# Two-layer conditioned FFN on one core: first stage rearranged between ScalarE, GpSimd and VectorE, last weights quantised earlier

## The chip, the cores and the metric

The kernel runs on one core of a Trainium2 chip. The metric is the device time in microseconds of one execution. Each time of a kernel is a median of several executions. A profiled execution is shown with its own time beside it: the span of the trace is a little shorter than the time.

The engines are called TensorE (PE in rows), VectorE (DVE), ScalarE (ACT), GpSimd (POOL) and SyncE (SP, which issues most transfers here). Each has its own instruction queue, executes it in order, and waits on semaphores for the others.

## The reference

x is 128 x 32 x 128 (tokens b, steps t, features c). Four parts follow each other:

1. **Conditioned linear layer**: `out = x W_base^T + b_base`, plus eight low-rank terms (rank 16) weighted by `cond_8` and scaled by 2.
2. **Layer norm, quantised activation and ternary weights**: `xn = (x - mean) * rsqrt(var + 1e-5) * gamma + beta`. The quantisation takes the maximum of |xn| over **all** tokens, divided by 127: nothing behind it can start before all of xn is there. The weights are replaced by `alpha * sign(w)` where |w| is over 0.7 of its mean.
3. **Mixture of experts**: softmax over `cond_8`, the best two of eight experts per token b, each a gated MLP (128 to 512 to 128, gelu), plus one shared MLP for all tokens.
4. **Quantised gated FFN** (128 to 384 to 128): weights in blocks of 32 rounded to 4 bits with their own scale, activations rounded to 16 bits with a scale from the maximum over all values, several times over.

x is added back after part 2 and after part 4. The result is float32.

## The kernel before, in words

The work is written out by hand for each engine (`@block.tensor`, `.vector`, `.scalar`, `.gpsimd`, `.sync`), and the order on each engine is the order of the code. There is no planner. `w.wait_ge(semaphore, count)` is the only link between engines. Even on one engine an operation that reads a predecessor's result waits on its semaphore (`step` counts such results in `d_rt`, `after` waits for them).

**Split values.** Products of float32 are made from `fp32r` halves: `hi` is a rounding copy of the value, `lo = value - hi`, and a product is `hi*hi + hi*lo + lo*hi`. Each weight of the experts (16 pieces of 128 x 512, two per expert) and of the shared MLP (three pieces) is loaded into one of eight staging slots `stg`, split once (`SPLITS`, L250, gives the number of pieces per round), and the 16 expert pieces are stored to a scratch in DRAM (`wscr`, L1745) from a ring of five buffers `wst`. Before, ScalarE made each `hi` (L1372, semaphore `a_whi`) and GpSimd each `lo` (L1601, `k_wlo`). SP waits for each `k_wlo` to store the piece and to reload its slot (L1742 to L1755). The eight down matrices arrive in `wdr`; ScalarE copies them to `WD` (`down_high`, L1331, rounds given by `WDS`), GpSimd makes their low halves (`down_low`, L1605).

**First stage (rounds n = 0 to 11).** Eight blocks of four steps t (128 x 512 values) go through a pipeline with one round per block. In round n TensorE transposes block n, makes the product `z` of block n-2, the low-rank product of block n-1 (`hidden`), the variance of block n-2 and the broadcast of the reciprocal deviation of block n-3. VectorE makes the low half of x (`narrow`), the weighted low-rank values (`hidden`), the maximum of block n-4, the variance plus epsilon (`ST`) and the product of block n-3. ScalarE squares, scales and shifts. GpSimd raises ST to the power -0.5 (L1587), and then makes its halves. Between these, VectorE computes the routing: from two counting products in `bank[6]` it derives the slots of all tokens (`KS`, `RT`, `Pm`, `tmpP`), the list of tiles (`etA` to `etI`) and the thresholds of the ternary weights (`tpos`, `tneg`). Before, most of the routing stands in rounds 2 to 4.

**Barrier.** The maximum of all blocks is reduced on VectorE, turned on TensorE (`turn_max`), reduced again (`top`) and spread (`spread_max`). `busy(k, ...)` are products whose result nobody reads. After that ScalarE rounds xn block by block (`round_xn`, which waits for `d_sc`), and a second pipeline (steps j = 0 to 11) makes the ternary product, adds x, transposes and starts the shared MLP for the first eight of its 32 units. Three products of 128 x 480 give the position table and the slot weights (`p_tab`, L527 to L530), which VectorE copies to `colI` and `Wt` in step 2 (L1048 to L1052). The buffers of the shared MLP (`Gb`, `HbS`) lie over `wst`; those of the transposed x (`XT`) over `stg`.

**Expert tiles and the rest of the shared MLP.** Twenty tiles of 12 or 16 token slots follow (two halves each): GpSimd gathers columns of x (`fetch`, L1622), TensorE makes gate and up products (`unit`) and down products. Then the other 24 shared units (n = 8 to 33). In these, VectorE and GpSimd quantised the last weights `WQ` (VectorE: scale, n = 10 to 12; GpSimd: L1653 to L1661), before TensorE turns them in `WTURN`. `LARGEST` gives the unit in which the maximum of each block is taken.

**Last stage.** The quantised FFN with its maxima over all values (`turn_max` 1 to 5).

## Time and profile before

| | |
|---|---|
| median of 3 runs | 398.12 us (396.21 to 399.63) |
| profiled execution | 397.88 us, span 396.2 us, mean granted clock 0.948 |
| TensorE matmuls, weight loads | 347.5 us (88%), 286.0 us (72%) |
| VectorE | 330.3 us (83%) |
| ScalarE | 262.1 us (66%) |
| GpSimd | 238.9 us (60%) |
| DMA | 47.77 MB, mean 121 GB/s |

Busy shares are averages over stages with different limits. The matmul and the weight load of TensorE overlap. A group of rows names the line of the instruction; L767, L1318 and L1557 are helpers that issue most operations of their engine, so the tiles (out <- in) say what an operation is. "Granted clock" is TensorE's, as a share of 2.4 GHz: 0.5 is 1.2 GHz. In brackets stands how long the engine stood idle before an instruction, and what ended that.

### The profile page before, as it was taken

Reading aid. Unit: us, or ns where it says so; the run is one execution under the profiler, and the core shown is the slowest. Engines: PE = TensorE matmul, PEld = TensorE weight load, DVE = VectorE, ACT = ScalarE, POOL = GpSimd, SP = SyncE. Lnnn points to the kernel's source line nnn. Section 1 sums busy time; section 2 is a strip of 40 time slices with the busy share of each in tenths; the row PEclk is TensorE's granted clock in tenths of the full one; section 3 lists DMA queues with packets and bytes.
Section 4 is the critical chain, followed back from the end, with each engine's and each line's share of the span. In section 5 each row is a group of like instructions: output and inputs, shape, how many; then the busy total and the mean of one; then the engine's idle time right before and its main releaser. Section 6 shows DMA issues by size and latency. Waiting matters only on the chain.

```text
span 396.2 us, 6229 instructions
## 1 busy us (share of the span) xinstructions
PE 347.5 (88%) x1759; PEld 286.0 (72%) x1759; DVE 330.3 (83%) x695; ACT 262.1 (66%) x344; POOL 238.9 (60%) x404
## 2 busy tenths in 40 slices
PE   7988977999999999999999999899999992035997
PEld 6765754768998998989898887688677661022797
DVE  4498667984899999989999989866669699989894
ACT  3656678966656566565756655455556899999760
POOL 2546795897557383756566115832179499994552
PEclk9898999999999999999999999999999996556999
DMA  5997994965244353433532003200000000000022
GB/s 152 346 409 269 331 336 135 296 187 213 106 151 170 112 209 107 174 146 117 201 110 106 2 2 113 100 2 0 1 2 0 1 1 0 0 2 0 1 108 106
DMA packets 19850, 47.77 MB, mean 121 GB/s; under 512 B 2787, under 2 KB 8934, under 8 KB 17254
## 3 DMA queue, kind: packets, MB, share of 16 engines
q1 hardware_dynamic: 18342, 47.16, 34.1%
q10 hardware_dynamic: 1472, 0.20, 0.3%
q8 instruction: 14, 0.23, 0.2%
q14 instruction: 22, 0.18, 0.1%
HBM read 33.10 MB, written 12.58 MB: 115 GB/s over the span
## 4 chain that ended last, share of the span: by engine, by line
PE 56%; POOL 15%; DVE 11%; issue 6%; DMA 5%; ACT 3%; SPq 1%; POOLq 1%; ACTq 0%; DVEq 0%
PE ps L396 55%; POOL G L1698 2%; POOL G L1554 2%; POOL WD L1557 2%; POOL XCh L1554 2%; POOL t L1554 2%; DMA wscr<-wst 2%; DVE O_i L773 2%; DVE unread L1275 2%; DMA wdr<-n_L_cond_skill_down_dram 2%; DMA bsr<-in_L_cond_Bs_dram 1%; PE ps L393 1%; DVE Hl L767 1%; POOL Hl L1557 1%; SPq L1728 1%
## 5 line engine op out<-in xcount | busy, mean ns | idle before, releaser
L1638 POOL CAST xg<-XT 128x64 fp32r x264 | 81.5, 358 | 52.5 <-DVE Hl L767 25.4
L396 PE MATMUL ps<-xg,Wr 128*128 128x384 f32 (+1 forms) x480 | 98.5, 353 | 1.3 <-POOL xg L1638 0.8
L396 PEld LDWEIGHTS ps<-xg,Wr 128*128 128x128 f32 x480 | 85.7, 188 | 8.4 <-POOL xg L1638 1.1
L1318 ACT ACTIVATE Hh<-HbS 128x512 fp32r<-128x512 f32 (+2 forms) x72 | 56.5, 785 | 47.6 <-DVE HbS L767 47.4
L767 DVE TENSOR_TENSOR HbS<-Gb,ps 128x512 f32<-128x512 f32 (+2 forms) x72 | 63.2, 878 | 21.8 <-PE ps L396 18.7
L1318 ACT ACTIVATE Gb<-ps 128x512 f32<-128x512 f32 (+2 forms) x72 | 54.1, 751 | 30.7 <-PE ps L396 28.9
L767 DVE TENSOR_TENSOR Hl<-HbS,Hh 128x768 fp32r<-128x768 f32 (+2 forms) x57 | 59.2, 1038 | 3.5 <-ACT Hh L1318 3.0
L773 DVE SCALAR_TENSOR_TENSOR C<-ps,Wt,C 128x32 f32 x264 | 52.4, 279 | 2.9 <-PE ps L396 2.6
L396 PE MATMUL ps<-XT,SHh 128*128 128x512 f32 x128 | 45.7, 399 | 0.8 <-DVE XT L767 0.4
L1557 POOL TENSOR_TENSOR Hl<-HbS,Hh 128x512 fp32r<-128x512 f32 x15 | 19.5, 1298 | 38.5 <-ACT Hh L1318 38.3
L396 PE MATMUL ps<-Hh,WT 128*128 128x384 f32 (+1 forms) x160 | 37.3, 355 | 0.0
L1318 ACT ACTIVATE ps<-G,S 128x1024 int32<-128x1024 f32 (+3 forms) x35 | 33.3, 987 | 5.4 <-DVE O_i L773 4.2
L396 PEld LDWEIGHTS ps<-Hh,WT 128*128 128x128 f32 x160 | 29.0, 188 | 2.1
L396 PE MATMUL ps<-WFh 128*128 128x512 f32 x30 | 11.4, 516 | 21.1 <-DVE S L776 11.8
L396 PEld LDWEIGHTS ps<-XT,SHh 128*128 128x128 f32 x128 | 24.0, 188 | 6.0 <-issue 0.7
L776 DVE TENSOR_REDUCE S<-G 128x1 f32<-128x1024 f32 (+2 forms) x25 | 28.1, 1166 | 0.3
L1557 POOL TENSOR_TENSOR wst<-stg,wst 128x512 fp32r<-128x512 f32 x16 | 20.6, 1306 | 7.7 <-ACT wst L1318 7.7
L396 PE MATMUL ps<-XT,SHl 128*128 128x512 f32 x64 | 25.0, 391 | 0.0
L396 PEld LDWEIGHTS ps<-WFh 128*128 128x128 f32 x30 | 6.2, 234 | 24.8 <-DVE S L1275 12.1
L396 PE MATMUL ps<-Hl,WT 128*128 128x384 f32 (+1 forms) x80 | 23.1, 370 | 0.2 <-DVE Hl L767 0.2
L396 PEld LDWEIGHTS ps<-WFd,G 128*128 128x128 f32 x192 | 21.7, 192 | 0.9 <-issue 0.9
L396 PE MATMUL ps<-WFd,G 128*128 128x128 f32 x192 | 22.0, 276 | 0.4 <-POOL G L1554 0.3
(223 smaller groups left out, 705.8 us busy)
## 6 DMA issues: line engine op xcount, KB each, us to landing
Wr<-wscr SPq DMA_DIRECT2D x20, 1024.0 KB, 4.9
wscr<-wst SPq DMA_DIRECT2D x16, 512.0 KB, 5.4
stg<-n_L_cond_skill_gate_dram SPq DMA_DIRECT2D x8, 256.0 KB, 6.2
stg<-in_L_cond_skill_up_dram SPq DMA_DIRECT2D x8, 256.0 KB, 6.6
wdr<-n_L_cond_skill_down_dram SPq DMA_DIRECT2D x8, 256.0 KB, 6.1
xscr<-X SPq DMA_DIRECT2D x8, 256.0 KB, 6.1
X<-xscr SPq DMA_DIRECT2D x8, 256.0 KB, 4.4
out_dram<-X SPq DMA_DIRECT2D x7, 256.0 KB, 2.0
```

The lines of the kernel that those rows point to most:

```text
L393: return e.transpose(o_, i_, identF[:, :])
L396: return e.matmul(o_, l, r, start=start, stop=stop, skip_group_check=True)
L767: return e.tensor_tensor(o_, a, b, op)
L773: return e.scalar_tensor_tensor(out=o_, in0=a, scalar=s, in1=b, op0=op0, op1=op1)
L776: return e.tensor_reduce(o_, i_, X, op, apply_absolute_value=absv)
L1275: return e.tensor_tensor_reduce(out=unread[:, p % 2, HALF[h]], in0=sloti(p % 3)[:, HALF[h]], in1=UA[:, p, HALF[h]], scale=1.0, scalar=0.0, ...
L1318: return e.activation(o_, i_, func, **kw)
L1554: return e.tensor_scalar(o_, a, s1, s2, op0, op1)
L1557: return e.tensor_tensor(o_, a, hi.bitcast(F32), SUB)
L1638: last = e.tensor_copy(xg[:, i % XR, :, T * s:T * s + T].rearrange("p a t -> p a t"), XT[:, :, :, bass.ds(regs[s - a_], 1)].rearrange("p a ...
L1698: e.tensor_tensor(Gi[:, pc(p)], Gi[:, pc(p)], t32[:, pooled_nth(f"t{p}") % 2, :], MUL).then_inc(k_y, 1)
L1728: e.dma_start(stg[:, n % 8, :], (sg, su)[n % 2][n // 2]).then_inc(s_stg[n % 8], 16)
```

## The change

- **Splits**: in rounds 1 to 8 twelve pieces (2, 2, 1, 2, 1, 2, 1, 1), both halves on GpSimd, with its own new semaphore `k_whi`. The last seven pieces are split in rounds 9, 10 and 11 (2, 3, 2), high half on ScalarE as before.
- **Down matrices**: their high halves move from rounds 8, 10, 11 and the steps i = 3 to 5 to the steps i = 0 to 5 after the barrier. The transfers have semaphores of their own (`s_wd`).
- **Routing**: the same operations, spread over rounds 3 to 10, ahead of `hidden` of their round. Two table operations with 480 columns (`tmpP`, `iof`) move from GpSimd to VectorE; tmpQ moves to round 10.
- **Table products** stand ahead of the barrier's products, and four instead of eight unread products follow. `colI` is copied between the two reduces of the barrier, `Wt` in step 0.
- **Waits**: rounding waits for the reciprocal alone (`d_inv`). The transposed x waits for single splits instead of all of them on VectorE, not at all on ScalarE.
- **Last weights**: VectorE makes all of their quantisation but one product ahead of the first expert tile, and that product in unit 16.
- **Elsewhere**: the low half of unit 30 is made after the hidden values of unit 31, the maximum of block 6 a unit later, and five unread products ahead of the fourth maximum are gone.

The diff, cut to its core (the routing operations that move are the same text at another place; their new place is given by the round):

```diff
-        SPLITS = (0, 2, 2, 2, 2, 2, 2, 2, 2, 3, 0, 0)
-        LARGEST = {10: 0, 12: 1, 14: 2, 18: 3, 22: 4, 26: 5, 31: 6, 33: 7}
-        WDS = {8: (0,), 10: (1, 2), 11: (3, 4)}
+        SPLITS = (0, 2, 2, 1, 2, 1, 2, 1, 1, 2, 3, 2)
+        NP = sum(SPLITS[:9])
+        LARGEST = {10: 0, 12: 1, 14: 2, 18: 3, 22: 4, 26: 5, 32: 6, 33: 7}
+        WDS = {0: (0,), 1: (1, 2), 2: (3,), 3: (4, 5), 4: (6,), 5: (7,)}
 ... TensorE
-                if n == 6:
+                if n == 8:
                     w.wait_ge(d_place, 2)
                     mm(bank[6][0:1, 0:NSLOT], bcF[:, :], Pm[:, :]).then_inc(p_route, 1)
-                if n == 8:
+                if n == 10:
                     w.wait_ge(d_parts, 2)
                     w.wait_ge(d_ord, 1)
 ...
+            w.wait_ge(d_tab, 1)
+            w.wait_ge(d_var, 8)
+            mm(bank[4][0:1, 0:NSLOT], ones[:, 0:1], tmpQ[:, :]).then_inc(p_tab, 1)
             w.wait_ge(a_zg, 8)
-            busy(8, bank[2], WbTh[:, :], xTh[:, 0, :])
+            w.wait_ge(d_sel, 2)
+            mm(bank[3][:, 0:NSLOT], ones[:, :], tmpP[:, :], True, False)
+            mm(bank[3][:, 0:NSLOT], ones[:, :], iof[:, :], False, True).then_inc(p_tab, 1)
+            busy(4, bank[2], WbTh[:, :], xTh[:, 0, :])
             turn_max(0, bank[6], S[:, 180:181])
             busy(1, bank[2], WbTh[:, :], xTh[:, 0, :])
             spread_max(0, bank[6])
-            (the three table products)
 ... shared_up, shared_down
-                w.wait_ge(k_wlo, NR)
+                w.wait_ge(k_wlo, NR - 1)
 ...
+                w.wait_ge(k_wlo, NR)
 ...
-            w.wait_ge(d_my, 10)
-            busy(5, bank[7], WFh[:, 0, :], WFh[:, 0:4, :].rearrange("p k c -> p (k c)"))
             turn_max(4, bank[7], col(MX2))
 ... VectorE, rounds: routing per round, ahead of hidden(n - 1)
+            3: n_, n_b, n_a (KS)         4: three sums of KS, RT 0 to 2
+            5: RT 3, 4, 6, 5, 4, 5       6: RT 5, 5, 7, S 48, S 56, sum S 42
+            7: bcF, tmpP, Pm             8: tsc, sum, tmpP (d_sel)
+            9: iof (d_sel), ordI        10: tmpQ (d_tab)
+            behind the product of their round: etC 4; tpos, tneg 5; etA, etC, etF 6;
+            tsc, tpos, sum 7; etA, etF, etI 8; tern, alpha 10
 ... VectorE, barrier
             top(0, bank[6])
-            w.wait_ge(k_tab, 1)
-            stt(tmpQ[:, :], vneg[:, :], bcF[:, :], Pm[:, :], ADD, MUL).then_inc(d_tab, 1)
+            w.wait_ge(p_tab, 1)
+            tt(colI[:, :], bank[4][0:1, 0:NSLOT], vneg[0:1, :], SUB).then_inc(d_tab, 1)
 ...
-            step(e.reciprocal(S[:, 183:184], S[:, 182:183]))
+            e.reciprocal(S[:, 183:184], S[:, 182:183]).then_inc(d_inv, 1)
 ...
                     w.wait_ge(a_xt, i + 1)
+                    if i >= 2:
+                        w.wait_ge(k_wlo, min(NG - 1 + i, NR))
                     low(x_half(1, i), bank[5 + i % 3], x_half(0, i)).then_inc(d_xt, 1)
-                if j == 2:
+                if j == 0:
                     w.wait_ge(p_tab, 2)
                     cp(Wt[:, :], bank[3][:, 0:NSLOT]).then_inc(d_tab, 1)
 ... VectorE, ahead of the expert tiles
+            w.wait_ge(s_wq, 48)
+            e.tensor_reduce(Sb, w9, X, ALU.max, apply_absolute_value=True).then_inc(d_bits, 1)
+            ts(Sb, Sb, 1.0 / 7.0, 1e-12, MUL, ALU.max); e.reciprocal(S[:, 104:140], Sb)
+            tt(w9, w9, wide(S[:, 104:140]), MUL); ts(WQ[:, :, :], WQ[:, :, :], RM, RM, ADD, SUB)
 ... VectorE, shared units
-                if n == 31:
-                    shared_low(30)
-                (scale of WQ at n = 10, 11, 12)
+                if n == 16:
+                    w.wait_ge(d_bits, 5)
+                    tt(w9, w9, wide(Sb), MUL).then_inc(d_bits, 1)
 ... ScalarE
-            split = 0
+            split = NP
-                for _ in range(SPLITS[n]):
+                for _ in range(SPLITS[n] if n >= 9 else 0):
 ...
-                w.wait_ge(d_sc, QSC)
+                w.wait_ge(d_inv, 1)
                 do(xnT[:, cols(j)], xnT[:, cols(j)], ACT.Identity, scale=S[:, 183:184], bias=RMC).then_inc(a_q, 1)
 ...
-                    w.wait_ge(k_wlo, NR)
                     do(x_half(0, i), bank[5 + i % 3]).then_inc(a_xt, 1)
-                    if 3 <= i < 6:
-                        down_high(2 + i)
+                    for k in WDS.get(i, ()):
+                        down_high(k)
 ... GpSimd
-                    w.wait_ge(a_whi, split + 1)
+                    if split < NP:
+                        w.wait_ge(s_stg[split % 8], 16 * (split // 8 + 1))
+                        if split >= WRING:
+                            w.wait_ge(s_wst[split % WRING], 16 * (split // WRING))
+                        e.tensor_copy(hi, stg[:, split % 8, :]).then_inc(k_whi, 1)
+                        w.wait_ge(k_whi, split + 1)
+                    else:
+                        w.wait_ge(a_whi, split + 1 - NP)
                     low(lo, stg[:, split % 8, :], hi).then_inc(k_wlo, 1)
 ...
+            w.wait_ge(k_wlo, NR)
             w.wait_ge(d_tab, 3)
             w.wait_ge(p_tab, 2)
             e.memset(C[:, 0:8 * DW], 0.0).then_inc(k_zero, 1)
 ... GpSimd, shared units
-                (the two products and the rounding of WQ at m = 12, 14, 16)
```

## Rows read from the trace of the kernel before

**Rows 1.** Windows: busy us (instructions) per engine, granted clock, DMA share, GB/s.

```profile
26.00:33.40 7.40, 4.80 (x31) 3.70 (x29) 7.33 (x36) 3.87 (x7) 3.89 (x3) 0.99 0.76 298
33.40:40.50 7.10, 7.10 (x32) 4.37 (x31) 6.00 (x14) 3.65 (x6) 3.51 (x3) 0.77 0.95 317
40.50:44.90 4.40, 4.31 (x28) 3.23 (x26) 3.13 (x6) 3.60 (x6) 3.94 (x4) 1.00 0.97 326
```

**Rows 2.** TensorE's timeline: start, busy us, work, [idle before <- releaser].

```profile
31.09 1.05 PE L396 MATMUL ps<-KC,sq 128*128 128x1 f32 x8 [2.60 <-ACT sq L1318]
```

**Rows 3.** ScalarE's timeline, first stage, round 5.

```profile
29.74 0.72 ACT L1318 ACTIVATE xnT<-xnT,S 128x512 f32<-128x512 f32 x1 [2.87 <-DVE xnT L767]
```

**Rows 4.** GpSimd's timeline, first stage: round 2, last power.

```profile
17.79 2.51 POOL L1557 TENSOR_TENSOR wst<-stg,wst 128x512 fp32r<-128x512 f32 x2
...
53.18 1.01 POOL L1587 TENSOR_TENSOR ST<-ST,KC 128x4 f32<-128x4 f32 x1 [0.57 <-DVE ST L770]
```

**Rows 5.** Groups by form, GpSimd, whole span: busy us, mean ns.

```profile
L1638 POOL CAST xg<-XT 128x64 fp32r x264 | 81.5, 358 | 52.5 <-DVE Hl L767 25.4 <-PE ps L396 19.8 <-issue 7.0
L1557 POOL TENSOR_TENSOR wst<-stg,wst 128x512 fp32r<-128x512 f32 x16 | 20.6, 1306 | 7.7 <-ACT wst L1318 7.7
...
L1554 POOL TENSOR_SCALAR XCh<-C,S 128x512 fp32r<-128x512 f32 x8 | 8.2, 1032 | 9.2 <-DVE S L770 9.2
L1587 POOL TENSOR_TENSOR ST<-ST,KC 128x4 f32<-128x4 f32 x8 | 8.1, 1014 | 14.3 <-DVE ST L770 14.3
...
L1554 POOL TENSOR_SCALAR tmpP<-iof,S 128x480 f32<-128x480 f32 x1 | 2.0, 1982 | 0.0
...
L1554 POOL TENSOR_SCALAR vneg<-vint 128x480 f32<-128x480 int32 x1 | 0.6, 594 | 0.0
```

**Rows 6.** VectorE's timeline, first stage, routing.

```profile
18.21 0.88 DVE L767 TENSOR_TENSOR KS<-S 128x8 f32<-128x8 f32 x1
```

**Rows 7.** ScalarE's timeline around the barrier.

```profile
55.29 1.14 ACT L1318 ACTIVATE WD<-wdr 128x512 fp32r<-128x512 f32 x2
...
59.58 0.63 ACT L1318 ACTIVATE WD<-wdr 128x512 fp32r<-128x512 f32 x1 [1.52 <-DMA wdr<-n_L_cond_skill_down_dram]
60.23 1.28 ACT L1318 ACT_TABLE_LOAD   x1
...
61.63 2.91 ACT L1318 ACTIVATE xnT<-xnT,S,S 128x512 f32<-128x512 f32 x4
```

**Rows 8.** TensorE's timeline around the barrier.

```profile
55.15 2.07 PE L396 MATMUL ps<-xTh,WbTh 128*128 128x512 f32 x8
58.09 0.27 PE L393 MATMUL ps<-identF,S 128*1 128x128 f32 x1 [0.86 <-DVE S L776]
...
61.16 0.97 PE L396 MATMUL ps<-iof,ones 128*128 128x480 f32 x2
```

**Rows 9.** VectorE's timeline behind the barrier: position tables.

```profile
66.39 0.63 DVE L767 TENSOR_TENSOR colI<-ps,vneg 1x480 int32<-1x480 f32 x1
66.96 0.64 DVE L764 COPY Wt<-ps 128x480 f32<-128x480 f32 x1
```

**Rows 10.** VectorE's timeline, first expert tile and shared phase.

```profile
86.71 1.47 DVE L767 TENSOR_TENSOR Hl<-HbS,Hh 128x512 fp32r<-128x512 f32 x2
91.94 0.96 DVE L767 TENSOR_TENSOR HbS<-Gb,ps 128x768 f32<-128x768 f32 x1 [3.76 <-PE ps L396]
...
238.53 1.35 DVE L1162 TENSOR_REDUCE S<-WQ 128x36 f32<-128x1152 f32 x1
...
249.66 3.14 DVE L767 TENSOR_TENSOR Hl<-HbS,Hh 128x512 fp32r<-128x512 f32 x1
```

**Rows 11.** TensorE's timeline, shared phase and its end.

```profile
252.86 0.50 PE L396 MATMUL ps<-Hl,SD 128*128 128x512 f32 x1 [1.35 <-DVE Hl L767]
...
284.88 0.73 PE L396 MATMUL ps<-Hh,SD 128*128 128x512 f32 x2 [0.75 <-ACT Hh L1318]
```

**Rows 12.** SP's queue: the last scratch store.

```profile
52.64 0.83 SPq L1745 DMA_DIRECT2D wscr<-wst  x1
```

More of the change, by code:

```diff
@@ L192, in program @@
         s_wst = [sem(f"s_wst{i}") for i in range(WRING)]
+        s_wd = [sem(f"s_wd{i}") for i in range(E)]
         s_wr = [sem(f"s_wr{i}") for i in range(3)]
@@ new lines, in _ @@
+                if n == 4:
+                    n_cum = n_a
+                    for k in range(3):
+                        after(n_cum)
+                        n_cum = step(tt(KS[:, k + 1, :, 4:12], KS[:, k, :, 4:12], KS[:, k, :, 4 - 2 ** k:12 - 2 ** k], ADD))
+                    after(n_cum, n_a)
+                    n_1 = step(stt(RT[:, 0, :], KS[:, 0, 0, 4:12], -16.0, S[:, 72:80], MUL, ADD))
+                    n_2 = step(tt(RT[:, 1, :], KA, KS[:, 0, 0, 4:12], SUB))
+                    n_3 = step(tt(RT[:, 2, :], KB, KS[:, 0, 1, 4:12], SUB))
@@ new lines, in _ @@
+                if n == 5:
+                    after(n_1, n_2, n_3)
+                    n_1 = step(ts(RT[:, 3, :], RT[:, 0, :], 12.0, -28.0, ALU.is_ge, MUL))
+                    n_2 = step(ts(RT[:, 4, :], RT[:, 0, :], 24.0, -28.0, ALU.is_ge, MUL))
+                    n_3 = step(tt(RT[:, 5, :], KA, RT[:, 2, :], ADD))
+                    n_8 = step(stt(RT[:, 6, :], RT[:, 1, :], 16.0, S[:, 72:80], MUL, ADD))
+                    after(n_1, n_2)
+                    n_2 = step(tt(RT[:, 4, :], RT[:, 3, :], RT[:, 4, :], ADD))
+                    after(n_3)
+                    n_3 = step(ts(RT[:, 5, :], RT[:, 5, :], -16.0, 16.0 * (NT - 1), MUL, ADD))
@@ new lines, in _ @@
+                if n == 6:
+                    after(n_2, n_3)
+                    n_3 = step(tt(RT[:, 5, :], RT[:, 5, :], RT[:, 4, :], ADD))
+                    after(n_3)
+                    n_3 = step(stt(RT[:, 5, :], RT[:, 0, :], 0.0, RT[:, 5, :], ALU.is_ge, MUL))
+                    after(n_3, n_8)
+                    n_3 = step(tt(RT[:, 7, :], RT[:, 5, :], RT[:, 6, :], ADD))
+                    after(n_3)
+                    step(tt(S[:, 48:56], S[:, 48:56], RT[:, 7, :], MUL))
+                    n_off = step(tt(S[:, 56:64], S[:, 56:64], RT[:, 7, :], MUL))
+                    after(n_off)
+                    n_tmp = step(red(S[:, 42:44].rearrange("p (k a) -> p k a", a=1),
+                                     S[:, 48:64].rearrange("p (k e) -> p k e", k=2), ADD))
@@ new lines, in _ @@
+                if n == 7:
+                    w.wait_ge(k_const, PART)
+                    cp(bcF[:, :], bcI[:, :]).then_inc(d_place, 1)
+                    after(n_tmp)
+                    n_tmp = step(ts(tmpP[:, :], iof[:, :], S[:, 42:43], None, ALU.is_equal))
+                    after(n_tmp)
+                    stt(Pm[:, :], iof[:, :], S[:, 43:44], tmpP[:, :], ALU.is_equal, ADD).then_inc(d_place, 1)
+                if n == 8:
+                    w.wait_ge(d_parts, 1)
+                    n_ = step(tt(tsc[:, :], tpos[:, :], fwr[:, :], MUL))
+                    w.wait_ge(d_rt, n_)
+                    red(S[:, 47:48], tsc[:, :], ADD).then_inc(d_parts, 1)
+                    w.wait_ge(d_place, 2)
+                    ts(tmpP[:, :], iof[:, :], S[:, 42:43], S[:, 38:39], ALU.is_equal, MUL).then_inc(d_sel, 1)
@@ L857, in _ @@
+                if 2 <= n and n - 1 < 8:
+                    hidden(n - 1)
                 if n == 2:
-                    hidden(1)
                     w.wait_ge(a_rows, 2)
@@ L995, in _ @@
                     ts(ST[:, i % 2, 0:4], AV[:, 0:4], 1.0, 1e-5, MUL, ADD).then_inc(d_var, 1)
[L996 to L1004 removed]
+                scaled(n - 3)
@@ new lines, in _ @@
+                if n == 7:
+                    after(n_)
+                    n_ = step(tt(tsc[:, :], tpos[:, :], tneg[:, :], ADD))
+                    step(tt(tpos[:, :], tpos[:, :], tneg[:, :], SUB))
+                    after(n_)
+                    red(S[:, 46:47], tsc[:, :], ADD).then_inc(d_parts, 1)
+                if n == 8:
+                    after(n_5, n_7)
+                    n_5 = step(tt(etA[:, WIDE:16], etA[:, WIDE:16], etF[:, WIDE:16], SUB))
+                    after(n_5)
+                    n_5 = step(tt(etA[:, WIDE:16], etA[:, WIDE:16], etB[:, WIDE:16], MUL))
+                    step(cp(etF[:, 0:WIDE], etA[:, 0:WIDE]))
+                    after(n_5)
+                    n_et = step(tt(etF[:, WIDE:16], etF[:, WIDE:16], etA[:, WIDE:16], ADD))
@@ L1007, in _ @@
                     ts(etI[:, 1, 0:NT], etF[:, 0:NT], 128.0, None, MUL).then_inc(d_et, 1)
+                if n == 10:
+                    w.wait_ge(p_route, 4)
+                    n_ = step(ts(S[:, 140:141], bank[6][:, 18:19], 1.0, None, ALU.max))
+                    cp(tern[:, :], bank[6][:, 384:512]).then_inc(d_tern, 1)
+                    after(n_)
+                    n_ = step(e.reciprocal(S[:, 141:142], S[:, 140:141]))
+                    after(n_)
+                    n_alpha = step(tt(S[:, 142:143], S[:, 141:142], bank[6][:, 19:20], MUL))
             w.wait_ge(d_mx1, 9)
@@ L1373, in _ @@
                     split += 1
-                for k in WDS.get(n, ()):
-                    down_high(k)
             do(S[:, 11:12], S[:, 13:14], ACT.Gelu_apprx_tanh)
```

218 lines of the change are left out of this document (66 added, 152 removed).

## The prediction

> **What bounds the kernel now.** I read the page's slices first (TensorE is busy almost throughout, except near 30 us and after 285 us), then the windows of the first stage, then each engine's timeline there, and last the waits at the places that the diff touches.
>
> The first stage sends eight blocks of x through rounds 0 to 11 and ends in a maximum over all tokens. The windows [rows 1] show one undisturbed round, 40.50 to 44.90: 4.40 us, TensorE busy 4.31 of it, VectorE 3.13. Four transposes more make it about 4.8 in the rounds that still load a block. The two rounds ahead of it last 7.40 and 7.10 us. In the first of them VectorE is busy 7.33 us: the routing of that round is one burst of small operations. In the second TensorE's granted clock is 0.77, a mixture of 2.4 and 1.2 GHz, just after TensorE has stood idle for 2.60 us [rows 2]. The chain of that idle time is visible: ScalarE waited 2.87 us for VectorE's product [rows 3], and TensorE for ScalarE's square. So some 14.5 - 2 x 4.8 = 4.9 us of the first stage are the price of the burst.
>
> From 94 us to 220 us TensorE is the bound and the change touches nothing.
>
> **Part by part.** *GpSimd takes both halves of 12 splits.* GpSimd starts its round-2 splits at 17.79 and the last power of the rounds at 53.18, done at 54.19 [rows 4]. Between them, in the new schedule, lie 10 split pairs (2,1,2,1,2,1,1 over rounds 2 to 8) and seven powers. A low half is 1.31 us, a power 1.01 [rows 5]. The trace has no plain 128x512 copy to fp32r on GpSimd. From below: a 480-element scalar operation with one input, 0.59. From above: the 480-element one with comparison, 1.98; the strided gather copies, 0.36 for 64 elements, point as high. Nearest, same width and fp32r output: XCh, 1.03 [rows 5]. I take 1.03, plus 0.15 for the wait on its own result. A pair is 2.5, so 10 x 2.5 + 7 x 1.01 = 32.1, and the last power is done at 17.79 + 32.1 = 49.9 instead of 54.2. GpSimd would allow 4.3 us of gain; at 0.59 it would allow all 4.9, at 1.98 it makes the rounds 5.2 us longer.
>
> The GPSIMD Engine Reference of the Trainium skill (section 4.1, Engine selection) advises against such elementwise work on GpSimd for two inputs and calls one input roughly line-rate; its section 3.1 measured 769 ns for 512 elements. By that price, an estimate from the page, the pairs would be 0.26 shorter and GpSimd would not bind at all. No row here shows that operation.
>
> *Routing spread, VectorE beside a fuller GpSimd.* VectorE's own routing work stays, some 13.3 - 2 x 2.5 = 8 us in the two long rounds, now spread over rounds 3 to 10, where about 2 us are free in each. What the spread gives up is GpSimd's silence: the burst ran while GpSimd was waiting. An operation of VectorE with two SBUF inputs that meets a GpSimd instruction ends only when that one ends: the 128x8 minimum at 18.21 took 0.88, until GpSimd's first low half of 17.79 was over [rows 4, 6]. With GpSimd nearly always busy, one such operation passes per GpSimd piece of about 1.2. Round 5 has six and follows a round of two splits: its block is about 2.4 us late, 1.8 of it beyond the slack of 0.6 that the undisturbed round shows between these steps and TensorE. Rounds 3 and 7 (three and two ahead of the block's product) cost 0.2 and 0.9. The rounds that follow one split cost nothing, as GpSimd is through before VectorE needs the port. Sum 2.9. Bounds: none, if they fit in the gaps that GpSimd's own waits leave; all 4.9, if each is held. The rounds give **-4.9 + 2.9 = -2.0 us** (-4.9 to +0).
>
> The same rule has a statement in the GPSIMD Engine Reference (section 1, Specifications): GpSimd's SBUF interfaces are shared with VectorE, with contention for instructions with two SBUF inputs or in a 2-port mode. The trace agrees (0.88 us for eight elements).
>
> *Table products ahead of the barrier.* TensorE is done with the rounds at 55.15 and now has three products of 0.9 (last row 0.97 [rows 8]) and four warm-up products (half of 2.07) before the turn: 55.15 + 2.75 + 1.03 = 58.9, where the turn stood at 58.09. ScalarE's third split of round 10 delays the last shift by 0.5 (two pieces were 1.14 [rows 7]), which lies beside this. Cost 0.8.
>
> *WD halves behind the barrier.* The first rounding waited until 61.63, since ScalarE stood 1.52 us for a wdr transfer, copied it at 59.58 and loaded its table for 1.28 after that [rows 7]. Now two splits (1.1) follow the last shift at 57.8, the table is loaded by 60.3, and the reciprocal is ready at 60.3 too. First rounding at 60.4: **-1.2 us**, the 0.8 included (-0.4 to -1.8).
>
> *colI and Wt.* They sat in VectorE's third step, 0.63 and 0.64 [rows 9]. colI goes into the wait for the maximum, Wt behind the first qT, where about half of it lies in a wait for ScalarE: **-0.7** (-0.3 to -1.2).
>
> *Eight WD copies on ScalarE instead of three, and the quantiser.* Steps 2 and 4 of the pipeline after the barrier get two copies; ScalarE had no slack in step 4, so its high halves, GpSimd's low halves and the first gather come about 0.7 late. Beside this VectorE does the whole quantiser where it had 3.76 us idle ahead of the first expert product at 91.94 (its last low half ends at 88.18 [rows 10]). The reduce is 1.35 [rows 10]; two products and a rounding over as many elements some 0.7 to 1.3 each, small ones 0.3, gaps 0.4, holds 0.5: about 4.9, until 93.1. Both delays overlap: **+1.2** (0 to +2.5), since TensorE has no idle time after it.
>
> *Shared phase.* GpSimd's quantiser goes. It had held VectorE's low half at 249.66 for 3.14 us instead of about 0.7, and TensorE stood 1.35 for it [rows 10, 11]; two smaller holds of the kind cost some 0.4. The one product left for VectorE is covered by its idle time there. **-1.7** (-1.2 to -2.1).
>
> *Its end.* The last product no longer queues behind a low half, so ScalarE's last high half is earlier; TensorE had waited 0.75 for it [rows 11]: **-0.8** (-0.3 to -1.2). The reduce of block 6 moves behind the last low half, still ahead of the last sum. The five warm-up products removed before the fourth maximum ran beside VectorE's reduces: 0. SP's queue keeps its order, later by GpSimd's lag; d_inv and the scalar multiply: 0.
>
> Sum: -2.0 - 1.2 - 0.7 + 1.2 - 1.7 - 0.8 = -5.2. The profiled execution took 397.88, the median is 398.12, 0.24 above. 397.9 - 5.2 = 392.7, as a median 392.9.
>
> **Rivals.** (1) *GpSimd's copy is slow*, near 1.98 [rows 5], decisive from about 1.46, where GpSimd's chain ends at 54.2 as before. Then the rounds cost +5.2 instead of -2.0, and holds by pieces of 2 us add 1 to 3 more: 392.9 + 7.2 + 2 = 402.1, slower. For it: the gather copies' price per element. Against it: XCh. Chance 0.08.
> (2) *The port eats the gain of the rounds*: every two-input operation held, rounds 0, first expert tile +2.0: 392.9 + 2.0 + 0.8 = 395.7. For it: 0.88 for a tiny operation; GpSimd's load rises by 12 copies. Against it: a late VectorE leaves GpSimd idle, which frees the port. Chance 0.24.
> (3) *The last scratch store lands late.* Gb and HbS lie over wst, and the store of split 15 is issued about 4 us later (it was at 52.64 [rows 12]) behind a fuller queue. A landing after 64 would hold the first gelu by up to 3: 394.5 to 396. Chance 0.08.
>
> **How the numbers follow.** The forecast has the remaining 0.60. The sum of all good ends is -11, which needs a copy of 0.6 us and no hold; I set the low end at 388.5. The high end, 399, covers rivals 2 and 3 with their bad ends and half of rival 1. The forecast's own range is 388.5 to 395.5. About 1% (4.0 us) is what a measurement of this kernel tells from no change: faster below 394.1. Forecast mostly there (0.54), a little of rivals 2 and 3 (0.07): faster 0.61; slower, most of rival 1's upper half, 0.05; the rest, 0.34, within 1%.
>
> **What would show it.** GpSimd's wst copies near 1.03 (0.6 or 2.0 decide rival 1). Rounds of 4.8 to 6.6 us, the one of round 5 longest, no granted clock under 0.9 from 30 to 40 us. The turn about 2 us before 58.9; the first rounding directly at the reciprocal. VectorE busy without a break from its last shared low half to the first expert product, and TensorE idle before the second half tile. In the shared phase no hold above 1.4 us. It is wrong if two-input operations of VectorE stand in rows of 1 us and more in every round, or if the first gelu follows a store.

## The result and the profile after

The changed kernel takes 393.84 us in the median of 6 runs (391.80 to 399.21), the kernel before, timed beside it, 397.99 (396.21 to 399.63): a ratio of 0.9888, 95% interval 0.986 to 0.9917, faster by 1.1%. One of the six executions, 399.21, was in a slower state of the chip, and the ratio leaves it out (median of the other five 393.60). Its profiled execution took 392.61 with a span of 390.9, 5.3 less than the span of before. The forecast was 392.9, with 0.61 on faster by over 1%.

The page of the changed kernel, total busy time and the slices (40 equal ones, tenths; PEclk is the granted clock of TensorE):

```profile
PE 343.6 (88%) x1750; PEld 284.8 (73%) x1750; DVE 336.0 (86%) x700; ACT 254.7 (65%) x332; POOL 234.3 (60%) x411
...
PEclk9999998999999999999999999999999996555999
```

VectorE is busier (330.3 before), ScalarE and GpSimd less (262.1, 238.9): what GpSimd took on (twelve copies) is less than what it gave up (two table operations, three of the quantiser's).

One more profile is needed to read the rest: the kernel before, profiled once more (e5 below, called the control here). Times of events in us; z(i) is the first conditioned product of block i, the third unit is the first group of 12 expert products in one piece (at 93.19 after), turn(1) and turn(5) are the transposes of the second and the last maximum.

| event | before | control | after |
|---|---|---|---|
| z(0) | 12.85 | 10.96 | 11.27 |
| z(7) | 49.28 | 46.51 | 43.91 |
| maximum over all tokens | 57.87 | 57.35 | 53.33 |
| first rounding | 61.63 | 60.66 | 55.89 |
| first shared product | 66.53 | 65.49 | 61.88 |
| first expert gate product | 89.55 | 88.43 | 85.67 |
| third unit | 95.89 | 94.79 | 93.19 |
| turn(1) | 287.81 | 286.61 | 282.00 |
| first output product | 371.15 | 370.18 | 365.90 |
| span | 396.2 | 395.2 | 390.9 |

Windows of the changed kernel, which answer to [rows 1]: us, busy us (instructions) of TensorE, its weight loads, VectorE, ScalarE and GpSimd, granted clock, DMA share, GB/s:

```profile
24.41:29.24 4.83, 4.75 (x31) 3.65 (x30) 4.83 (x17) 2.63 (x4) 4.38 (x5) 1.00 0.80 316
29.24:34.07 4.83, 4.75 (x32) 3.66 (x30) 4.69 (x15) 2.67 (x4) 3.20 (x4) 1.00 0.94 304
34.07:38.46 4.39, 4.31 (x28) 3.21 (x26) 4.29 (x10) 2.67 (x4) 3.67 (x5) 1.00 0.45 144
38.46:43.91 5.45, 5.41 (x29) 3.20 (x28) 5.38 (x13) 1.96 (x3) 4.33 (x4) 1.00 0.92 298
...
56.00:58.00 2.00, 0.40 (x4) 0.23 (x4) 1.26 (x3) 2.00 (x3) 2.00 (x2) 1.00 1.04 376
58.00:62.00 4.00, 3.13 (x17) 2.41 (x18) 3.37 (x6) 2.32 (x5) 1.82 (x3) 0.57 1.10 335
```

The long rounds are gone: TensorE is busy 98 or 99% of each of these four, at 2.4 GHz. The 5.45 us of the fourth hold a routing product (Pm and bcF) that the change moved there from an earlier round. Before, it stood in the round of 7.10 us (first line before, second after):

```profile
36.67 0.96 PE L396 MATMUL ps<-Pm,bcF 128*1 128x480 f32 x2
...
40.51 0.97 PE L398 MATMUL ps<-Pm,bcF 128*1 128x480 f32 x2
```

Round 5, for which the prediction reckoned the longest holds, is the window of 24.41 to 29.24. These are its six routing operations on VectorE's 128x8 tables:

```profile
26.27 0.22 DVE L770 TENSOR_SCALAR RT<-RT 128x8 f32<-128x8 f32 x2
26.42 1.26 DVE L767 TENSOR_TENSOR RT<-KS,RT 128x8 f32<-128x8 f32 x1
27.61 0.15 DVE L773 SCALAR_TENSOR_TENSOR RT<-RT,S 128x8 f32<-128x8 f32 x1
27.68 0.57 DVE L767 TENSOR_TENSOR RT<-RT 128x8 f32<-128x8 f32 x1
28.18 0.15 DVE L770 TENSOR_SCALAR RT<-RT 128x8 f32<-128x8 f32 x1
```

One was held for 1.26 us, to the end of GpSimd's low half of 26.35, one for 0.57; the others passed at once. The price has moved: behind the barrier TensorE is busy 0.40 of 2 us, and the next 4 us run at 0.57, nearly all at 1.2 GHz.

GpSimd's timeline: the new copy, then the end of its first stage (start, busy us, line, work, tile, count, [idle before <- releaser]):

```profile
16.18 0.61 POOL L1603 CAST wst<-stg 128x512 fp32r<-128x512 f32 x1
16.87 1.27 POOL L1561 TENSOR_TENSOR wst<-stg,wst 128x512 fp32r<-128x512 f32 x1
...
48.10 1.01 POOL L1591 TENSOR_TENSOR ST<-ST,KC 128x4 f32<-128x4 f32 x1 [0.17 <-DVE ST L770]
49.07 5.41 POOL L1561 TENSOR_TENSOR wst<-stg,wst 128x512 fp32r<-128x512 f32 x4
54.42 2.51 POOL L1561 TENSOR_TENSOR SHl<-stg,SHh 128x512 fp32r<-128x512 f32 x2
56.87 1.48 POOL L1561 TENSOR_TENSOR SD<-stg,SD 128x512 fp32r<-128x512 f32 x1
58.41 1.17 POOL L1619 MEMSET C<- 128x1088 f32 x1
```

The copy takes 0.61, not 1.03, and the last power of the rounds is done at 49.11, against 54.19 before [rows 4]. But seven low halves and the zeroing follow without a gap until 59.58, across the barrier. VectorE behind the barrier, changed kernel:

```profile
56.74 0.48 DVE L770 TENSOR_SCALAR qT<-xnT 128x512 bf16<-128x512 f32 x1 [0.77 <-ACT xnT L1325]
57.13 0.65 DVE L764 COPY Wt<-ps 128x480 f32<-128x480 f32 x1
57.70 0.93 DVE L770 TENSOR_SCALAR qT<-xnT 128x512 bf16<-128x512 f32 x1
...
61.74 1.53 DVE L770 TENSOR_SCALAR qT<-xnT 128x512 bf16<-128x512 f32 x1
```

The same operation takes 0.42 where GpSimd has no such work (e6, e12). The first tile, VectorE and then TensorE, which answer to [rows 10]:

```profile
84.22 1.34 DVE L1067 TENSOR_REDUCE S<-WQ 128x36 f32<-128x1152 f32 x1
85.60 1.30 DVE L770 TENSOR_SCALAR S<-S 128x36 f32<-128x36 f32 x1
86.94 0.38 DVE L1071 RECIPROCAL S<-S 128x36 f32<-128x36 f32 x1
87.35 1.44 DVE L767 TENSOR_TENSOR WQ<-WQ,S 128x1152 f32<-128x1152 f32 x1
88.82 0.76 DVE L770 TENSOR_SCALAR WQ<-WQ 128x1152 f32<-128x1152 f32 x1
89.85 0.95 DVE L767 TENSOR_TENSOR HbS<-Gb,ps 128x768 f32<-128x768 f32 x1 [0.27 <-issue]
```

```profile
85.67 3.54 PE L398 MATMUL ps<-xg,Wr 128*128 128x384 f32 x18 [0.81 <-POOL xg L1645]
90.86 1.34 PE L398 MATMUL ps<-xg,Wr 128*128 128x384 f32 x6 [1.65 <-DVE HbS L767]
```

Before, VectorE had 3.76 us idle here [rows 10], and TensorE did its 24 gate and up products in one piece.

### The profile page after: what moved, and what is told of

It is laid out like the page before. It is cut to its first block, busy times and chain, and to the rows that moved or that the text cites. A ratio compares the mean times of both kernels' runs of the same rounds, so it can differ in the third digit from the quotient of the medians.

```text
span 390.9 us, 6212 instructions
## 1 busy us (share of the span) xinstructions
PE 343.6 (88%) x1750; PEld 284.8 (73%) x1750; DVE 336.0 (86%) x700; ACT 254.7 (65%) x332; POOL 234.3 (60%) x411
## 4 chain that ended last, share of the span: by engine, by line
PE 60%; DVE 18%; POOL 11%; issue 5%; ACT 3%; DMA 1%; DVEq 0%; ACTq 0%; POOLq 0%
PE ps L398 58%; POOL G L1696 2%; DVE S L776 2%; POOL G L1558 2%; POOL XCh L1558 2%; POOL t L1558 2%; DVE O_i L773 2%; PE ps L395 1%; DMA wbr<-in_L_cond_W_base_dram 1%; DVE qT L770 1%; DVE HbS L767 1%; DVE Hl L767 1%; DVE X L773 1%; DVE xnT L767 1%; DVE C L773 1%
## 5 line engine op out<-in xcount | busy, mean ns | idle before, releaser
L767 DVE TENSOR_TENSOR Hl<-HbS,Hh 128x768 fp32r<-128x768 f32 (+2 forms) x57 | 55.5, 973 | 2.1 <-ACT Hh L1325 1.8
L1558 POOL TENSOR_SCALAR G<-O_i 128x1536 f32<-128x1536 int16 (+2 forms) x13 | 12.7, 979 | 16.4 <-DVE O_i L773 16.0
L1561 POOL TENSOR_TENSOR wst<-stg,wst 128x512 fp32r<-128x512 f32 x16 | 21.4, 1345 | 1.0
L1325 ACT ACTIVATE WT<-WD 128x1024 fp32r x20 | 21.0, 1049 | 0.0
```

What stands on the lines that cost most here:

```text
L767: return e.tensor_tensor(o_, a, b, op)
L1325: return e.activation(o_, i_, func, **kw)
L1558: return e.tensor_scalar(o_, a, s1, s2, op0, op1)
L1561: return e.tensor_tensor(o_, a, hi.bitcast(F32), SUB)
```

## The experiments

All but e5 differ from the changed kernel by the edit shown, which is cut to its core. "Against the changed kernel" compares profiled spans where nothing else is said.

**e1, high halves on ScalarE.**

```
-        SPLITS = (0, 2, 2, 1, 2, 1, 2, 1, 1, 2, 3, 2)
-        NP = sum(SPLITS[:9])
+        SPLITS = (0, 2, 2, 2, 2, 2, 2, 2, 2, 3, 0, 0)
+        NP = 0
...
-                for _ in range(SPLITS[n] if n >= 9 else 0):
+                for _ in range(SPLITS[n]):
```

> The changed kernel with ScalarE making every high half again, two pieces a round as before; all else of the change stays (routing spread, table products ahead of the barrier, WD copies behind it, early quantiser). Theory 1 (the two long rounds were VectorE's burst; GpSimd's copies only free ScalarE in the start-up): first conditioned product at about 12.9 us instead of 11.3, rounds of 4.8 us still without a long one, last VectorE maximum about 1 to 1.6 us later than 53.3; time +0.5 to +1.6 against the changed kernel's 393.8. Rival (the move of the high halves to GpSimd is what shortened the rounds): two rounds of over 6 us come back, maximum near 57, time +3 to +4.

397.63 us, ratio 0.9987 (0.9961 to 1.0013), +3.8 in the medians; the execution profiled was one of the longer ones (399.97). Without this part the change gains nothing that the runs can tell from zero. From z(0) to z(7) it is 35.93 us instead of 32.64 (35.92 in e6, which has the same rounds), z(0) stays at 11.06. No round is over 6 us; two are 5.84 and 5.92. ScalarE in this version, rounds 3 and 4:

```profile
22.01 0.63 ACT L1325 ACTIVATE wst<-stg 128x512 fp32r<-128x512 f32 x1 [2.42 <-DMA wscr<-wst]
...
26.12 0.63 ACT L1325 ACTIVATE wst<-stg 128x512 fp32r<-128x512 f32 x1 [0.61 <-DMA wscr<-wst]
```

ScalarE's copy waits for a scratch store to free the buffer, and the block's shifts and squares stand behind it in ScalarE's order; on GpSimd the same wait holds nothing of the block. The round before (5.84) has such a wait too, 1.48 us for a staging transfer. These two rounds are 2.1 of the 3.3 us; the rest is spread over the others. The control shows three waits for scratch stores (2.16, 0.24, 1.16 us). The first profile of before shows two (1.03, 0.76), and the rounds around them are still 4.8, so a shorter wait of this kind need not cost anything. And TensorE ahead of the turn, same version:

```profile
53.52 2.08 PE L398 MATMUL ps<-identF,ST 128*128 128x128 f32 x8 [0.75 <-POOL ST L1591]
55.52 1.76 PE L398 MATMUL ps<-tmpQ,ones 128*1 128x480 f32 x2
57.21 1.97 PE L398 MATMUL ps<-tmpP,ones 128*128 128x480 f32 x2
...
60.77 0.27 PE L395 MATMUL ps<-identF,S 128*1 128x128 f32 x1
```

VectorE's maximum was there at 57.27 + 0.16. The clock had fallen to 1.2 GHz, the table products took nearly double (0.96 and 1.07 in the changed kernel), and the turn came 3.3 us after the maximum.

**e2, routing in one burst**: VectorE's loop over the rounds has the routing in the order and rounds of the kernel before, and TensorE's two routing products stand at rounds 6 and 8 again; the selectors and tmpQ stay in rounds 8, 9 and 10.

```
-                if n == 8:
+                if n == 6:
                     w.wait_ge(d_place, 2)
...
-                if n == 10:
+                if n == 8:
                     w.wait_ge(d_parts, 2)
```

> The changed kernel with VectorE's routing in the order of before (one burst in rounds 2 to 4, and the two route products of TensorE in rounds 6 and 8); GpSimd keeps both halves of twelve pieces. Theory 1: the burst now meets a GpSimd that is nearly always busy and each two-input operation waits for a piece of it, so the long round is longer than the 7.4 us of before (8 to 11 us), the granted clock falls after it; last VectorE maximum 58 to 61 instead of 53.3, time +4 to +7, that is no better than before the change. Rival (the splits carried the gain, the order of the routing did not matter): maximum within 1.5 us of 53.3, time +0 to +1.5.

395.16 us, ratio 0.9944 (0.9913 to 0.9975). z(0) to z(7) is 35.36, the round of the burst 7.3 us. The theory's 8 to 11 us were not reached: during the burst GpSimd again stands idle, 3.50 us, until VectorE delivers its next variance (at 26.34). The time is as the rival had it, the maximum (55.52) lies between the two. So the burst alone costs 2.7 us of the rounds, ScalarE's splits alone 3.3, and both together, in the kernel before, 35.55 (control) and 36.43: they hide each other. Either part alone brings at most 1.1 us of the 2.9 to 3.8 that both bring.

**e3, only round 1's high halves on ScalarE.**

```
+                if n == 9:
+                    split = NP
-                for _ in range(SPLITS[n] if n >= 9 else 0):
+                for _ in range(SPLITS[n] if n == 1 or n >= 9 else 0):
```

> The changed kernel with only the two high halves of round 1 on ScalarE (as before). Theory (ScalarE's wait for the staging transfer stood in front of its copy of block 2, so all rounds started 1.6 us late before the change): ScalarE copies block 2 at about 12 instead of 10.35, first conditioned product at 12.7 to 12.9 instead of 11.27, last VectorE maximum 1.3 to 1.6 later than 53.3, time about +1.5. Rival (the earlier start is a difference in the arrival of the first transfers between two executions): first conditioned product stays within 0.4 us of 11.27.

One execution, 394.36. z(0) stays at 11.28: the early start does not come from these copies. The first tile began at 85.76, as in the changed kernel; after its wait of 1.67 us the granted clock was 0.68 (92 to 96 us), the group of six products took 2.17 instead of 1.34, and the third unit came 1.5 us later. The changed kernel had 1.00 there, behind the same wait; the edit does not touch this part.

**e4, the quantiser on VectorE inside the shared phase** (its six operations at steps 10, 11, 12, 13, 15 and 17, each as this one).

```
+                if n == 10:
+                    w.wait_ge(s_wq, 48)
+                    e.tensor_reduce(Sb, w9, X, ALU.max, apply_absolute_value=True).then_inc(d_bits, 1)
```

> The changed kernel with the whole quantiser of the last weights on VectorE inside the shared phase (units 10 to 17, one operation a unit, two of the large ones a unit apart), none ahead of the first expert tile. Theory 1 (ahead of the tile the block costs TensorE its 1.65 us of idle time before the second gate products; in the shared phase VectorE has 0.7 to 1.35 us idle in a unit and GpSimd holds nothing): first expert tile without that idle time, shared units unchanged at 2.04 us, time -1.1 to -1.6 against 393.8, near 392.4. Rival (the place of the early block is free, since something else delays the second half tile; late, it pushes shared units): TensorE idle before the second half tile stays over 1 us, or units 10 to 17 lose it again: time 0 to +1.

392.25 us, ratio 0.9885 (0.9857 to 0.9912), the same as the changed kernel's. The wait in the first tile is gone (VectorE idles 3.77 us there again) and the third unit is at 92.04, 1.15 earlier. But turn(1) is at 282.36, 0.36 later: what follows gives back 1.5. Half of it shows in TensorE's timeline:

```profile
243.66 0.50 PE L398 MATMUL ps<-Hl,SD 128*128 128x512 f32 x1 [0.38 <-DVE Hl L767]
252.52 0.50 PE L398 MATMUL ps<-Hl,SD 128*128 128x512 f32 x1 [0.38 <-DVE Hl L767]
```

So where the quantiser stands hardly matters in the sum: the wait that it leaves in one place turns up in another.

**e5, the control:** the kernel before, one execution.

> The kernel before once more, one look, as a control. Its profile put the first conditioned product at 12.85 us, while the changed kernel and every version of it so far had it between 11.06 and 11.28, also the one in which all high halves were back on ScalarE. Theory: the 1.6 us is a matter of this one profiled execution (its staging transfers came late), and the product will stand at 11.1 to 11.6 here, with the later events of the first stage 0 to 1.6 us earlier than in the first profile. Rival: the new routing order or the semaphores' set-up moves the start, and it stands at 12.8 again.

396.89 us, span 395.2; z(0) at 10.96. The windows of TensorE's start, first profile of before, then the control:

```profile
9.00:13.00 4.00, 4.00 (x19) 3.70 (x20) 1.48 (x6) 1.89 (x4) 1.51 (x2) 0.57 0.76 270
```

```profile
9.00:13.00 4.00, 3.69 (x21) 2.73 (x21) 1.30 (x5) 1.98 (x5) 2.03 (x2) 1.00 0.79 252
```

The expectation was near on the place (11.1 to 11.6) and had the wrong cause. In the first profile the staging transfer did land half a microsecond later (ScalarE's copy at 10.78 against 10.25), but TensorE did not wait for it: it was busy all 4 us from 9 to 13, nearly all at 1.2 GHz. Of the 5.3 us between the two first profiles, the 1.0 between before and control is therefore no work of the change. A late start doesn't survive whole: z(0) differs by 1.9 and the maximum by 0.5, since in the control ScalarE stood 2.49 us for the wdr transfer ahead of the last shifts (0.40 before).

**e6, e1 with the two wide table products behind the spread.**

```
+            spread_max(0, bank[6])
+            w.wait_ge(d_sel, 2)
+            mm(bank[3][:, 0:NSLOT], ones[:, :], tmpP[:, :], True, False)
+            mm(bank[3][:, 0:NSLOT], ones[:, :], iof[:, :], False, True).then_inc(p_tab, 1)
```

> The version with all high halves back on ScalarE, and in addition the two wide table products (selectors times ones, into bank 3) behind the spread of the maximum again, where they were before the change. With the splits on ScalarE TensorE idles so much in the rounds that its granted clock is 0.66 to 0.74 from 50 to 62 us, and the three table products took 1.76, 1.97 and 1.04 us where the changed kernel needs 0.96, 1.07 and 0.97; the turn stood 3.5 us behind VectorE's maximum. Theory (a product ahead of the turn is only cheap at 2.4 GHz): the turn comes 2 to 3 us earlier, the time is 394.6 to 396, -1.6 to -3 against 397.6. Rival (the turn is late for VectorE's maximum and ScalarE's table load): 397 to 398.

395.97 us, ratio 0.9961 (0.9933 to 0.9989), -1.7 against e1 in the medians, -1.0 by the ratios. The maximum is at 57.18 as in e1, the first rounding at 60.51 instead of 62.22. The intervals of the two overlap, so the gain in time is not clear of noise; the profiles show it. The forecast of 2 to 3 us was too high, the direction right: at 1.2 GHz the two products ahead of the turn cost 1.6 us from maximum to rounding, at 2.4 GHz (e7) 0.7.

**e7, the same move in the changed kernel** (the edit of e6 alone).

> The changed kernel with the two wide table products alone behind the spread again. Mine: they lie with the four warm-up products between 51.80 and the turn at 54.44, while VectorE's maximum was done at 53.49, so the turn comes up to 0.9 us earlier; but behind the spread they fill 1.8 us in which TensorE's clock otherwise fell to 0.59 (58 to 62 us), so that the time is 392.3 to 393.3, -0.5 to -1.5 against the changed kernel. Rival (Wt is copied from them and ordered between the first two qT, so their late end holds VectorE as before): 393.8 to 394.8, 0 to +1.

391.99 us, ratio 0.9876 (0.9819 to 0.9934), not told apart from the changed kernel's 0.9888; span -0.3. TensorE:

```profile
53.60 0.27 PE L395 MATMUL ps<-identF,S 128*1 128x128 f32 x1 [0.55 <-DVE S L776]
```

The turn follows the maximum at once (54.44 in the changed kernel), the first rounding is at 55.25, 0.64 earlier, and the granted clock stays at 1.00 behind the barrier. Still the first shared product is only 0.41 earlier, at 61.47: from rounding to shared product it is 6.22 us with a full clock. The lost clock was not what held that stretch.

**e8, the five warm-up products back** ahead of the fourth maximum.

```
+            w.wait_ge(d_my, 10)
+            busy(5, bank[7], WFh[:, 0, :], WFh[:, 0:4, :].rearrange("p k c -> p (k c)"))
```

> The changed kernel with the five unread products ahead of the fourth maximum back. In the profile of the changed kernel TensorE went through the last block's 17 products at half clock for longer, and the last 5 us from the second unit to the end lost 0.65 against before. Theory: without the five products the clock returns later; with them 393.2, -0.4 to -0.8. Rival (the prediction's 0: the clock's return is not tied to them): -0.1 to +0.3 against the changed kernel.

393.67 us, ratio 0.9885 (0.9841 to 0.9929): nothing, as the prediction had it. From the first of the 17 final products to turn(5) it was 7.12 us before, 7.44 in the control, 7.77 after, 7.55 here, and 7.12 in e12, which has no warm-up products. That stretch starts at 0.50 in all of them and ends when the clock comes back:

```profile
355.00:361.50 6.50, 6.50 (x13) 3.94 (x14) 6.50 (x11) 6.26 (x7) 0.14 (x1) 0.50 0.01 4
361.50:363.00 1.50, 1.50 (x6) 0.85 (x4) 0.53 (x3) 1.50 (x3) 0.00 (x0) 0.79 0.00 0
```

**e9, every copy of GpSimd twice.**

```
+                        e.tensor_copy(hi, stg[:, split % 8, :]).then_inc(k_dup, 1)
+                        w.wait_ge(k_dup, split + 1)
                         e.tensor_copy(hi, stg[:, split % 8, :]).then_inc(k_whi, 1)
```

> The changed kernel, but GpSimd makes each of its 14 high-half copies twice, the second after the first; the output is the same. A pair then costs about 0.61 + 0.1 + 0.61 + 0.1 + 1.28 = 2.7 us, a little over the 2.5 that the prediction took for it with a copy of 1.03. Theory A (the prediction's step, the step's size was off only because the copy was cheap): GpSimd is nearly always busy, VectorE's two-input operations are held as reckoned, and the span from the first to the last conditioned product is 34.5 us instead of 32.6 (the prediction's 36.4 - 2.0), the time +1.5 to +2.5 against the changed kernel. Theory B (the rounds are bound by TensorE at 4.8 us with slack on every other engine, so that holds were over-reckoned whatever the copy costs): 32.6 to 33.4, the time 0 to +0.8. With the last power of the rounds later (48.10, by up to 4) the maximum moves too under A, and by under 1 us under B.

(There are 12 copies, not 14.) 394.58 us, ratio 0.9949 (0.9921 to 0.9976); span +1.3. From z(0) to z(7) it is 32.98, 0.34 more than with single copies, and GpSimd no longer waits for anything from 12 to 54 us. Theory B holds for the rounds; the span is between the two theories. What is lost is lost behind them: the last shift's transposes wait 1.39 us for GpSimd's last power, and the first expert gate product comes at 87.37, 1.7 later.

**e10, e4 and e7 together.**

> The two best single edits together: the quantiser's six operations of VectorE inside the shared phase, and the two wide table products behind the spread. If their gains lie in different stretches, they add: in the profiles the second unit of the first tile came 1.1 us earlier by the first edit (0.4 to 0.5 of that was given back by two short waits near 243 and 252 us), and the first tile 0.4 us earlier by the second. So 391.4 to 391.9, -0.6 to -1.0 against the changed kernel in the sum of the profiles, ratio to before 0.983 to 0.986. Rival (the first tile's start is set elsewhere, and one edit hides the other): 392.2 to 392.8.

393.63 us, ratio 0.9907 (0.9881 to 0.9934): no better than either. In its profile z(0) is at 12.71, with a granted clock of 0.57 from 9 to 13 us, and all of the first stage is late by 1.4 to 1.6. The expected sum isn't shown. From the third unit to turn(1) it is 190.3 us as in e4, 1.5 more than in the changed kernel.

**e11, e10 with tmpQ behind the maximum.**

```
             red(S[:, 180:181], S[:, 183:192], ALU.max).then_inc(d_col, 1)
             top(0, bank[6])
-            w.wait_ge(p_tab, 1)
-            tt(colI[:, :], bank[4][0:1, 0:NSLOT], vneg[0:1, :], SUB).then_inc(d_tab, 1)
+            w.wait_ge(k_tab, 1)
+            stt(tmpQ[:, :], vneg[:, :], bcF[:, :], Pm[:, :], ADD, MUL).then_inc(d_tab, 1)
```

> The same with the table operation tmpQ (128x480, two SBUF inputs) behind the maximum over all tokens, where it was before the change, its product behind the spread and colI just ahead of Wt. In round 10 tmpQ was held by GpSimd's low halves and took 1.58 us ahead of the last block's reduce and product, and its product was one of three ahead of the turn. Theory (it lies on the path to the maximum): the maximum comes 0.6 to 1.2 us earlier, the rounding 0 to 0.8 earlier, since tmpQ then stands ahead of the scale, and the first shared product is -0.4 to +0.4: the time is even with the version without this edit, 391.3 to 392.3. Rival (GpSimd is quiet there, tmpQ takes 0.7 inside the wait for the spread): 390.8 to 391.2.

393.88 us, ratio 0.9916 (0.9886 to 0.9945). The maximum is at 53.07, only 0.3 earlier than in e7, and the first shared product at 63.53, 2.06 later than there: with three table products behind the spread, at 0.50 of the clock from 56 to 58 us, colI and Wt stand at 59.20 and 59.78, ahead of the second qT. Both expectations were too good.

**e12, splits earlier on GpSimd**, with e7's move.

```
-        SPLITS = (0, 2, 2, 1, 2, 1, 2, 1, 1, 2, 3, 2)
+        SPLITS = (0, 2, 2, 2, 2, 1, 2, 2, 1, 1, 3, 1)
```

> The changed kernel with the two wide table products behind the spread, and with two splits moved forward on GpSimd: (0,2,2,2,2,1,2,2,1,1,3,1) instead of (0,2,2,1,2,1,2,1,1,2,3,2), so GpSimd makes 14 high halves and ScalarE five. In the changed kernel GpSimd idled about 2 us in each of rounds 3, 5 and 7, and its remaining low halves and the zeroing ran from 49.07 to 59.58, through the barrier, where VectorE's qT operations took 1.19, 0.93 and 0.64 us instead of 0.42. From the first rounding to the first shared product it is 6.2 us in the version without the earlier splits (4.8 to 4.9 in the kernel before, whose GpSimd was through its multiplications by 61 and waited). Theory (GpSimd's backlog behind the barrier is what costs 1.1 us there): its last low half ends at about 55.5 instead of 58.4, that stretch is 5.1 to 5.6, while the rounds, bound by TensorE, stay at 32.6 to 33.2 from the first to the last conditioned product; time 391.0 to 391.7, -0.6 to -1.2 against the version without. Rival (the stretch is set by ScalarE and the Wt copy, or the stores and staging transfers hold the earlier splits): the last low half ends after 57, the stretch is 6.0 or more, time 391.8 to 392.6.

391.04 us (390.90 to 392.93), ratio 0.983 (0.979 to 0.9871), span 389.2. It is the fastest version, 2.8 us under the changed kernel's median, 2.3 by the ratios. GpSimd and VectorE behind the barrier in e12:

```profile
54.99 1.27 POOL L1561 TENSOR_TENSOR SD<-stg,SD 128x512 fp32r<-128x512 f32 x1
```

```profile
56.40 0.43 DVE L770 TENSOR_SCALAR qT<-xnT 128x512 bf16<-128x512 f32 x1 [0.77 <-ACT xnT L1325]
...
57.54 0.42 DVE L770 TENSOR_SCALAR qT<-xnT 128x512 bf16<-128x512 f32 x1
```

GpSimd's last low half ends at 56.26 instead of 58.41, the qT operations take 0.43 and 0.42 instead of 1.19 and 0.93 in e7, and from the first rounding to the first shared product it is 5.19 us instead of 6.22. e6 agrees from another side: there the low halves were over at 57.17, ahead of the rounding at 60.51, qT took 0.43 and 0.42, and the stretch is 5.19 as well. The rounds take 33.42 instead of 32.69, so 0.7 is paid there, a little more than expected. The first expert gate product is at 84.54, 0.76 earlier than in e7; 0.3 of that is an earlier z(0), 10.98. Its interval overlaps that of the changed kernel's ratio a little (0.986 to 0.9871), so what is shown is that it beats the kernel before by 1.3 to 2.1%, and that the stretch behind the barrier is shorter.

## Why the prediction was right

The time was right to 1 us, and the sum partly by cancellation. Step by step (before and control against after, from the table):

- *The rounds*, -2.0 forecast. z(0) to z(7) took 36.43 (before) and 35.55 (control) and takes 32.64: -3.8 or -2.9. The undisturbed rounds of 4.8 and 4.4 came as forecast. Three terms were mis-sized. The 4.9 us to be gained held 1.1 that was not to be had: the routing product only moves, and its new round takes 5.45 instead of 4.39. Against the first profile the change gains all of the other 3.8. The copy costs 0.61, next to the low bound of the prediction (0.59), not 1.03. And the holds by GpSimd, priced at 2.9, cost next to nothing: even with GpSimd busy without a wait (e9) the rounds are only 0.34 longer. The step that failed is "one such operation passes per GpSimd piece": of round 5's six operations one was held for a whole piece, and the round, forecast as the longest, took 4.83. VectorE is busy all 4.83 us of it, but what is held fits into its slack. The GPSIMD Engine Reference of the Trainium skill (section 3.1, 769 ns for 512 elements) would have been nearer to the 0.61 of the trace than the row that the prediction took. By the page's price GpSimd would not bind, and it did not.
- The prediction ascribed all 4.9 us to the routing burst. e1 and e2 show two causes of about the same size, one behind the other: the burst (2.7), and ScalarE's copies (3.3), which wait for a staging transfer and for scratch stores ahead of the block's own work. The move of the high halves was counted only as load on GpSimd; without it the change gains nothing (e1).
- *z(7) to the maximum*: 8.59 before, 10.84 in the control, 9.42 after. The control's 10.84 hold the 2.49 us wait for wdr which the change removed. Against the first profile the stretch is 0.8 longer, which no term of the sum had; e11 gives back 0.36 of it (against e7), the rest is open.
- *The barrier*, -1.2 forecast for the first rounding against the maximum: 3.76 (control 3.31) became 2.56, -1.2 (-0.75). The turn was late by the table products as forecast; e7 takes 0.64 of that back.
- *colI and Wt*, -0.7 forecast; **nothing of it is seen.** First rounding to first shared product rose from 4.90 (4.83) to 5.99, +1.1. The prediction let GpSimd's low halves end with the rounds; they run through the barrier and hold the qT operations. Against e7, e12 takes 1.03 away by that alone. The 0.3 by which its 5.19 is still above 4.90 go with Wt's new place between the first two qT operations. What the two copies free lies behind the first shared product, where they stood before; no run measures it by itself.
- *WD copies and quantiser*, +1.2 forecast (0 to +2.5), both said to overlap. They add: the first gate product is 0.8 later relative to the shared phase (23.02 and 22.94 became 23.79), and the third unit another 1.18 behind it, where TensorE waits 1.65 for VectorE. +2.0.
- *Shared phase and its end*, -1.7 - 0.8 = -2.5 forecast: third unit to turn(1) went from 191.92 (191.82) to 188.81, -3.1 (-3.0). The stalls of 1.35 at 253 us and of 0.75 at the end [rows 11] are gone. That is read from the traces; no run undoes these two parts by themselves.
- *The rest*, 0 forecast: turn(1) to the first output product +0.56 (+0.33), in the stretch where the clock returns (e8).
- *The start*, not in the sum: -1.6 against the first profile, +0.3 against the control; the granted clock, not the change.

Against the control the spans differ by 4.3, the timed medians by 4.15. Rival 1 fell with the copy's 0.61. Rival 2 asked for no gain in the rounds; there was one of 2.9 or more. Rival 3 did not happen: the last scratch store was issued at 54.58 [rows 12], and the first gelu ran at 63.74, with no wait for a store.

Left open: why the ratio of e9 is worse than its profile (0.6% against 0.3%), and how often an execution of either kernel starts with the low clock; the timed runs show no clock.

## What to carry over

When work moves off an in-order engine, look at what it waits for there, not only at how long it takes: a copy of 0.63 us stood 2.4 us for a store, ahead of the critical work, and without its move the change gained nothing. Two causes in series hide each other, so undo each alone before one is given the whole price. And follow a loaded helper engine to its last instruction: a backlog that is harmless in a round bound by TensorE can cost behind the next barrier, here 1.0 us; use its idle rounds first, as e12 does.

## What was not expected of the hardware

- GpSimd copies 128x512 fp32 to fp32r in 0.61 us; the scalar operation of the same shape (XCh) takes 1.03 [rows 5].
- A one-input VectorE operation (qT, 128x512 to bf16) beside GpSimd's two-input work took 0.93 to 1.53 us; with no such work on GpSimd (e6, e12) 0.42 and 0.43, and 0.64 and 0.65 where it met most of the zeroing (59.22 after, 58.53 in e12).
- The granted clock fell to 0.57 in 58 to 62 us after TensorE had been busy 0.40 of 2 us, stayed at 1.00 there in e7 (0.82 of 2), and was 0.57 from 9 to 13 us in two profiles (before, e10), 1.00 in the control and the changed kernel. TensorE had been busy 2.13 and 2.41 of the 3 us ahead in the two low ones, 2.04 and 2.85 in the two others, so the rows don't tell them apart. About 1.5 us of an execution's first product hang on it.
